# Preparing the second image inside the first maximum pass, and loading x ahead of the weights, in a kernel of two attention layers

## The reference

```python
# layer 0
f = xf @ wf + bf; g = xf @ wg + bg; hh = xf @ wh + bh        # 8, 8 and 64 columns
attn = softmax(einsum('bnk,bmk->bnm', g, f)); o = einsum('bnm,bmc->bnc', attn, hh)
x = gamma * o + x
# layer 1
q, k, v = x @ Wq + bq, x @ Wk + bk, x @ Wv + bv              # 64 columns each
attn = softmax(einsum('bic,bjc->bij', q, k)); out = einsum('bmn,bmc->bnc', attn, v)
x = gamma * out + x
```

## Time and profile before

| | us |
|---|---|
| runs of the kernel before | 4221.15, 4228.95, 4231.31; median 4228.95 |
| profiled execution, its own time | 4228.57 |
| its span | 4226.4 |
| TensorE busy in the span | 4030.3 (95%) |
| VectorE, ScalarE, GpSimd busy | 3271.2, 3191.0, 1953.5 |
| first window of 100 us: TensorE busy | 40.24 |

### The profile page before, as it was taken

One profiled execution on the slowest core, in us unless ns is written; L12 is line 12 of the kernel. 1 busy time (PEld: TensorE's weight loads), 2 busy tenths in 40 slices (PEclk: granted clock), 3 DMA queues, 4 the chain that ended last, 5 costly groups with the idle time before them and its releaser, 6 DMA issues.

```text
span 4226.4 us, 84183 instructions
## 1 busy us (share of the span) xinstructions
PE 4030.3 (95%) x25681; PEld 1349.5 (32%) x25681; DVE 3271.2 (77%) x6298; ACT 3191.0 (76%) x5674; POOL 1953.5 (46%) x909
## 2 busy tenths in 40 slices
PE   4999999999999999999999999999999999999999
PEld 3223332233322333223332233323333233322333
DVE  3877887778877787777877788777887778877787
ACT  2466896778867788767986689776897678977788
POOL 3596106941089311992029910497105961079410
PEclk7799999999999999999999999999999999999999
DMA  1001000010000000000000000001000010000000
GB/s 33 1 1 31 1 1 11 1 31 1 1 12 11 21 1 11 1 11 21 1 12 1 18 14 1 11 1 31 1 1 12 1 31 1 1 11 3 30 1 11
DMA packets 15060, 41.88 MB, mean 10 GB/s; under 512 B 4068, under 2 KB 4068, under 8 KB 12260
## 3 DMA queue, kind: packets, MB, share of 16 engines
q1 hardware_dynamic: 14692, 36.96, 2.9%
HBM read 20.17 MB, written 8.39 MB: 7 GB/s over the span
## 4 chain that ended last, share of the span: by engine, by line
PE 84%; DVE 6%; issue 6%; ACT 3%; POOL 0%; SPq 0%; DVEq 0%; DMA 0%; ACTq 0%; POOLq 0%
PE sum_banks L480 23%; PE sum_banks L578 20%; PE score_banks L566 20%; PE score_banks L466 12%; PE sum_banks L502 3%; PE sum_banks L438 2%; DVE tile_max L922 1%; DVE o_tr L1089 1%; ACT e_whole L816 1%; PE score_banks L430 1%; DVE c_stack L949 1%; ACT g_tr L734 1%; PE sum_banks L415 1%; DVE k_low L969 0%; DVE x_mid L1140 0%
## 5 line engine op out<-in xcount | busy, mean ns | idle before, releaser
L816 ACT ACTIVATE e_whole<-score_banks,exp_bias,down 128x512 f32<-128x512 f32 x2048 | 1573.9, 773 | 249.8 <-DVE o_tr L1089 211.3
L922 DVE TENSOR_REDUCE tile_max<-sum_banks 128x1 f32<-128x512 f32 (+1 forms) x2128 | 1364.8, 685 | 444.0 <-PE sum_banks L438 440.5
L355 POOL TENSOR_TENSOR e_sum<-e_sum,e_whole 128x1024 f32<-128x1024 f32 x704 | 1659.5, 2357 | 83.0 <-ACT e_whole L752 31.9
L752 ACT ACTIVATE e_whole<-score_banks,no_bias,down 128x1024 f32<-128x1024 f32 x1024 | 1229.0, 1204 | 527.1 <-PE score_banks L466 516.1
L1089 DVE TENSOR_SCALAR_CACHE_REDUCE o_tr<-score_banks,neg_down 128x1024 f32<-128x1024 f32 x1024 | 1313.6, 1283 | 320.4 <-PE score_banks L566 281.4
L480 PE MATMUL sum_banks<-e_whole,proj 128*64 128x512 f32 x4096 | 1123.3, 626 | 0.0
L578 PE MATMUL sum_banks<-e_whole,v_scaled 128*64 128x512 f32 x4096 | 1066.7, 602 | 45.1 <-DVE v_scaled L1079 17.1
L566 PE MATMUL score_banks<-k_high,q_split 128*64 128x512 f16 x4096 | 810.2, 388 | 30.6 <-ACT e_whole L816 9.7
L566 PE MATMUL score_banks<-k_low,q_split 128*64 128x512 f16 x4096 | 799.2, 382 | 0.0
L438 PE MATMUL sum_banks<-f_tr,g_tr 33*128 33x512 f16 x2128 | 700.4, 402 | 19.0 <-DVE tile_max L922 14.6
L352 POOL TENSOR_TENSOR e_sum<-e_whole 128x1024 f32<-128x1024 f32 x32 | 75.4, 2357 | 1355.5 <-ACT e_whole L752 1355.5
(11 more groups left out here) (147 smaller groups left out, 1868.5 us busy)
## 6 DMA issues: line engine op xcount, KB each, us to landing
x_in<-in_x_dram SPq DMA_DIRECT2D x19, 1024.0 KB, 4.9
out_dram<-x_mid SPq DMA_DIRECT2D x32, 256.0 KB, 2.7
k_high<-k_high SPq DMA_DIRECT2D x32, 128.0 KB, 2.2
k_low<-k_low SPq DMA_DIRECT2D x32, 128.0 KB, 2.2
w<-in_L_conv_wg_dram SPq DMA_DIRECT2D x2, 2.0 KB
w<-in_L_conv_wf_dram SPq DMA_DIRECT2D x2, 2.0 KB
w<-in_L_conv_wh_dram SPq DMA_DIRECT2D x2, 16.0 KB
b<-in_L_conv_bh_dram SPq DMA_DIRECT2D x1, 32.0 KB
```

What stands on the lines that cost most here:

```text
L355: nc.gpsimd.tensor_tensor(acc, acc, e_whole[:, i % U0, :], ALU.add).then_inc(e_added, 1)
L752: nc.scalar.activation(e_whole[:, i % U0, :].rearrange("p (a n) -> p a n", a=2), score_banks[:, 2 * (i % 2):2 * (i % 2) + 2, :], ACT.Exp, ...
L816: nc.scalar.activation(e_whole[:, u, h * BANK:(h + 1) * BANK], score_banks[:, 2 * (u % 2) + h, :], ACT.Exp, bias=exp_bias[:, u:u + 1], sca ...
L922: nc.vector.reduce_max(tile_max[:, blk, j:j + 1], sum_banks[:, (2 + j % banks) % 4, :], AX_X).then_inc(a_used, 1)
```

## The change

x of image 0 is loaded first, ahead of the weights. TensorE turns it before it waits for the weights, and VectorE copies and scans it before it works on the weights (the function `weights` holds what stood at L867 to L884). VectorE makes the halves of image 0 right after the scan of image 1, and biases and scales image 1 after them. TensorE starts the maximum pass as soon as image 0's stack is turned. VectorE makes the halves of image 1 after four blocks of the pass; GpSimd, whose program is not changed, then fills the stacks; and TensorE turns them in units between the tiles of the last two blocks. ScalarE's program is not changed either.

```diff
+    UNIT_AT = BPC - 2
+    PIECES_AT = BPC // 2
...
+            load(0, 0)
             for col, w_, b_ in ((0, wg, bg), (CK, wf, bf), (GFW, wh, bh)):
...
-            load(0, 0)
...
+            def turn_image(image):
+                pe.wait_ge(x_loaded, 16 * loads(image, True))
+                for r in range(RT):
+                    turn_x(0, x_in, r, score_banks[:, r, :])
+            def project_image(image):
+                for r, pair in enumerate((pair_c, pair_d, pair_a, pair_b)):
+                    pe.wait_ge(xt_dve[0], image * RT + (r + 1 if r < 2 else RT))
+                    project0(r, pair)
+                pe.wait_ge(pj_act, (image + 1) * RT)
+                bound_of_qk(image, score_banks[:, 0, :])
             pe.wait_ge(ident_ready, 1)
+            turn_image(0)
             pe.wait_ge(const_ready, N_CONST)
             pe.wait_ge(w_in, 16 * N_W)
             pe.wait_ge(h_weighted, 2)
...
+            project_image(0)
+            pe.wait_ge(w1s_ready, 1)
+            turn_image(1)
+            project_image(1)
+            pe.wait_ge(w1s_ready, 2)
+            pe.wait_ge(f_stacked, 4)
+            pe.wait_ge(g_stacked, 4)
+            for n in range(UNITS):
+                if n >= 4:
+                    pe.wait_ge(unit_sb, n - 3)
+                turn_stack(n, score_banks[:, n % 4, :])
+            pe.wait_ge(unit_sb, UNITS)
+            for blk in range(BPC):
+                for j in range(ATN):
+                    max_pass_tiles((0, 0, 0), blk, [j], 4)
+                    if blk >= UNIT_AT and j % 2 == 1:
+                        n = (blk - UNIT_AT) * (ATN // 2) + j // 2
+                        if n == 0:
+                            pe.wait_ge(f_stacked, 8)
+                            pe.wait_ge(g_stacked, 8)
+                        if n >= 4:
+                            pe.wait_ge(unit_sb, UNITS + n - 3)
+                        turn_stack(n, score_banks[:, n % 4, :])
+            for blk in range(EARLY):
+                max_pass_tiles((0, 0, 1), blk, range(ATN), 4)
             pe.wait_ge(unit_sb, 2 * UNITS)
-            for chunk, blocks in ((0, BPC), (1, EARLY)):
-                for blk in range(blocks):
-                    max_pass_tiles((0, 0, chunk), blk, range(ATN), 4)
             first_max_rows()
...
             for image in range(2):
                 for r in range(RT):
                     turned_x(image, 0, r, score_banks[:, r, :])
                 scan_x(image)
-                fg_bias(image, image)
                 if image == 0:
+                    weights()
+                    fg_bias(0, 0)
                     fg_largest(0, 0)
-                scales(image, image, score_banks[:, 0, :])
-            for image in range(2):
-                if image == 1:
-                    fg_largest(1, 1)
-                    dve.wait_ge(f_stacked, 4)
-                    dve.wait_ge(g_stacked, 4)
-                fg_scales(image)
-                fg_scaled(image, image)
-                fg_high_part(image, image)
-                fg_rest(image, image)
...
-            with dve.Fori(0, BPC) as blk:
+                    scales(0, 0, score_banks[:, 0, :])
+            fg_scales(0)
+            fg_scaled(0, 0)
+            fg_high_part(0, 0)
+            fg_rest(0, 0)
+            fg_bias(1, 1)
+            fg_largest(1, 1)
+            scales(1, 1, score_banks[:, 0, :])
+            with dve.Fori(0, PIECES_AT) as blk:
+                block_max(0, blk, range(ATN), 4)
+            dve.wait_ge(f_stacked, 4)
+            dve.wait_ge(g_stacked, 4)
+            fg_scales(1)
+            fg_scaled(1, 1)
+            fg_high_part(1, 1)
+            fg_rest(1, 1)
+            with dve.Fori(PIECES_AT, BPC) as blk:
                 block_max(0, blk, range(ATN), 4)
             split_max(0, 0)
```

More of the change, by code:

```diff
@@ L865, in _ @@
             nc.vector.memset(bound_in[C:C1, :], 1.0).then_inc(const_ready, 1)
[L867 to L885, removed]
+            def weights():
+                dve.wait_ge(w_in, 16 * N_W)
+                dve.wait_ge(ident_ready, 1)
+                chain.link(nc.vector.tensor_scalar(w0[:, GFW:PW], w0[:, GFW:PW], gammas[:, 0:1], None, ALU.mult))
+                nc.vector.tensor_scalar(b0[:, GFW:PW], b0[:, GFW:PW], gammas[:, 0:1], None, ALU.mult).then_inc(h_weighted, 1)
+                chain.link(nc.vector.scalar_tensor_tensor(h_abs[:, :], w0[:, GFW:PW], -1.0, w0[:, GFW:PW], ALU.mult, ALU.max))
+                for a in range(2):
+                    rows = slice(a * C, (a + 1) * C)
+                    chain.count(nc.vector.tensor_tensor(mid_abs[rows, :], h_abs[rows, :], ident[rows, rows], ALU.add))
+                chain.link(nc.vector.tensor_scalar(hb_mul[:, :], hb_raw[:, :], gammas[0:C, 0:1], None, ALU.mult))
+                chain.link(nc.vector.scalar_tensor_tensor(bound_in[0:C, :], hb_mul[:, :], -1.0, hb_mul[:, :], ALU.mult, ALU.max))
+                nc.vector.scalar_tensor_tensor(wb_abs[:, :], wb_raw[:, :], -1.0, wb_raw[:, :], ALU.mult, ALU.max
+                                               ).then_inc(h_weighted, 1)
+                dve.wait_ge(coef_ps, 1)
+                nc.vector.tensor_copy(mid_t[:, :], sum_banks[0:C, 0, 0:P]).then_inc(coef_sb, 1)
+                dve.wait_ge(coef_ps, 2)
+                chain.count(nc.vector.reduce_max(x_coef[:, :], sum_banks[:, 1, 0:P], AX_X))
+                chain.link(nc.vector.reduce_max(b_coef_raw[:, :], sum_banks[:, 0, 0:P], AX_X))
+                nc.vector.tensor_scalar(b_coef[:, :], b_coef_raw[:, :], 2.0 ** -100, None, ALU.max).then_inc(coef_sb, 1)
@@ L1016, in _ @@
             dve.wait_ge(const_ready, N_CONST)
-            rebase(START)
             for image in range(2):
@@ L1021, in _ @@
                 scan_x(image)
-                fg_bias(image, image)
                 if image == 0:
+                    weights()
+                    fg_bias(0, 0)
                     fg_largest(0, 0)
-                scales(image, image, score_banks[:, 0, :])
-            for image in range(2):
-                if image == 1:
-                    fg_largest(1, 1)
-                    dve.wait_ge(f_stacked, 4)
-                    dve.wait_ge(g_stacked, 4)
-                fg_scales(image)
-                fg_scaled(image, image)
-                fg_high_part(image, image)
-                fg_rest(image, image)
-            assert chain.n == 2 * (LINK_PIECES + LINK_BOUND)
-            rebase(START + 2 * (LINK_PIECES + LINK_BOUND))
-            with dve.Fori(0, BPC) as blk:
+                    scales(0, 0, score_banks[:, 0, :])
[15 more added lines that the diff above has]
+            with dve.Fori(PIECES_AT, BPC) as blk:
                 block_max(0, blk, range(ATN), 4)
@@ L1041, in _ @@
                 block_max(1, blk, range(ATN), 4)
-            START += 2 * (LINK_PIECES + LINK_BOUND) + LINK_MAX
+            START = chain.n
             def image_steps(image, par):
```

## The result

The changed kernel takes 4204.6 us (median of 5, 4200.1 to 4208.5) against 4225.9 us before (median of 5), a ratio of 0.9948 with a 95% interval of 0.9934 to 0.9963. The forecast was 4201.5. The profiled execution has a span of 4202.5 us, 23.9 less than before.

What follows compares the result with a forecast made beforehand. The prediction took one long chain through TensorE, 95% busy, as the bound, so time saved before the first chunk stays saved. −30.65 + 2.9 + 0.7 = −27.05 us from 4228.57 gave 4201.5 us, own bounds 4196 to 4208, range 4194 to 4213.

Steps and rivals of the forecast that it cites:

- The front: Before the maximum pass: loading and turning x first starts projection 3.6 us earlier and image 0's stack 5.1 us earlier.
- GpSimd's switch back: GpSimd's return from the all-reduce to ordinary operations before image 0's stack: 6.8 us, bounds 5.96 to 8.26.
- start of the pass: The maximum pass begins at 62.8 us instead of 93.45, without waiting for image 1: 30.65 us earlier.
- The halves: After four blocks of the pass VectorE stops its reductions for image 1's halves: 2.9 us added, at most 3.8.
- Rival 1: In the pass, GpSimd's stack operations and VectorE's reductions exclude each other, adding 8.0 us: 4209.5 us; chance 12%.
- The transposes: Eight units of eight between tiles in the pass's last two blocks: 0.7 us added, bounds 0 to 2.4.
- The stack beside the pass: GpSimd finishes image 1's stack at 93.3 to 93.9 us, just before TensorE asks at 93.9; nothing added.
- Rival 2: Ahead of the pass: image 0's stack still starts at 51.2, so 5.1 us are not won: 4206.6 us; chance 10%.
- Rival 3: TensorE's clock stays low in the first chunks, about 28 us per chunk; two chunks give 4258.6 us; chance 3%.
- the mark: Start of the matrix product ending the first chunk's preparation, at 142.86 us before; forecast near 115.8.

Runs made afterwards that it cites:

- the pass alone: Changed kernel with its front put back in the old order and image 1 still in the maximum pass; ratio 0.9952 to the kernel before.
- the spread kernel: Changed kernel with image 1's halves after one block and a unit of transposes behind each sixth tile from the 30th; 4198.1 us, on repeat 4203.5 us.
- the front alone: Changed kernel with image 1's stack made and turned ahead of the maximum pass, as before; ratio 0.9987 to the kernel before.
- the changed kernel's second profile: The changed kernel measured again, unaltered, beside the other experiments; 4210.0 us, ratio 0.9957 to the kernel before.

## Why the prediction was right, and where it was not

*The front.* Forecast 3.6 us for the projection, measured 4.0: the last weight came 0.4 us earlier (18.11), for which I had left 0 to +1, the wrong side. GpSimd's switch back took 7.8 us where I took 6.8 from the one undisturbed row; so the stack started at 46.9 instead of 46.1. Over the runs the same idle time was between 7.7 and 9.0 us. The pass started at 63.58 (forecast 62.8).

*The sum, as measured.* −29.87 (start of the pass) + 0.42 (first reduction 0.96 us behind it instead of 0.54) + 3.55 (halves) + 4.46 (transposes) = −21.44. The 4.46 are the remainder: the 64 reductions take 46.33 us (64.54 to 110.87) where they took 38.36, 7.97 more, of which 3.55 are the halves; the other 0.04 lie between the last reduction and the mark. Forecast were −30.65 + 2.9 + 0.7. The 0.42 had no term in the forecast, and its cause stays open.

*The halves* were 0.65 us above my value and within its bound; the cause is the one I had named as the bound. I had put the exclusion of the two engines on GpSimd's side only, as 0.7 us of waiting. What the runs show is that it can fall on either. VectorE's low half took 1.57 us in all six profiles in which GpSimd's stack operation started within 0.02 us of it, and 0.69 where GpSimd came later or not at all. In the kernel of the pass alone, for image 0, the low half started 0.2 us ahead (50.44 against 50.66) and took 0.69; there GpSimd's pair took 2.38 us instead of 2.03. Which of two nearly simultaneous operations is held the recorded starts don't tell: VectorE's of 4.54 us stands 0.03 us ahead of GpSimd's and waited all the same. The trace agrees with the Trainium skill, "SBUF — State Buffer" (section "SBUF: two separate sides"), which names VectorE operations with two SBUF inputs; the one of 4.54 us has its two inputs from there, and the reductions from PSUM beside the same stack were not stretched. Rival 1 (they take turns for the whole stack) is therefore wrong: 20 reductions took 12.04 us while GpSimd worked.

*The transposes* are the term that was mis-sized: 0.7 forecast, 0 to 2.4 as bounds, 4.5 measured. Two steps of it failed. I let the clock rise once TensorE had no gaps; it stayed at 0.50 through 14.5 us of such work in the changed kernel (96.27 to 110.77), and through 22.8 us in the spread one (82.56 to 105.37). The Trainium skill, "TensorE: Matmul & The Clock Gate" (section "What's actually happening"), by whose rule I would have taken 0, would have been further off; where the page and the rows differ, the rows decide. And I priced transposes and tiles each at their own pace. In turn a unit takes 0.97 us (0.85 in a row of units: 55.86 to 56.71 in the changed kernel), two tiles 0.97 (0.85 by their columns), and six tiles 2.67 (83.53 to 86.20) where 6 × 0.427 are 2.56: about 0.11 us at each change between the two kinds, a price that the rows show and whose cause they don't. So two tiles and a unit are 1.93 us instead of 1.7, and eight times the difference to 1.20 is 5.9 instead of 4.1 (the forecast's 8 × 0.5, which is 4.0), of which 1.4 didn't reach VectorE, where I had left 2 for the filled banks.

*The stack beside the pass* was the step I called a hair's breadth; it held with 2.1 us to spare, since it started 0.5 us later and TensorE 2.4. *Rival 2* (front moves nothing) is wrong by the front alone. *Rival 3* (the clock low in the first chunk) happened a little: it rose some 16 us into the first chunk (which starts at 123.6) instead of 10,

```profile
135.00:140.00 5.00, 5.00 (x18) 0.85 (x16) 2.58 (x4) 2.08 (x2) 4.43 (x2) 0.52 0.00 0
140.00:145.00 5.00, 5.00 (x34) 1.27 (x32) 3.06 (x5) 2.94 (x4) 1.94 (x1) 1.00 0.01 3
```

and the first 30 us behind the mark had a mean clock of 0.69 against 0.79. It never came near the point from which it decides, a whole chunk at the lower level.

*Behind the mark.* The part behind it took, in twelve profiles, from 4073.2 to 4095.9 us (before 4083.5, after 4081.1), with no order by kernel. Two profiles of the spread kernel alone, with marks of 115.53 and 115.61, stand at 4074.5 and 4095.9. So no single median here could have settled a term of the sum. What causes the scatter stays open.

*What was luck.* The forecast gain was 27.05 us; the measured one is 21.44 at the mark and 21.24 by the medians, so the forecast was 5.6 to 5.8 us off. That 4201.5 came out only 3.1 us below 4204.6 is owed to its base: I took the gain off the profiled execution, 4228.57, which lies 2.7 us above the median of five, 4225.85. The mechanism was right (image 1 out of the way, GpSimd's switch ahead of the stack of image 0, a pause for the halves); the price of the transposes was not, and the nearness of the time doesn't speak for it.

## What to carry to other kernels

Work that waits on another engine's slow start belongs inside a stretch that doesn't need it: here moving image 1 into the pass gave 17.7 of 21.4 us. Once it is there, count the host engine's time anew. Transposes between the tiles are nearly free only where the tiles and the unit together fit the other engine's pace (six tiles and a unit nearly did, 3.64 us against 3.59; two tiles and a unit didn't, 1.93 against 1.20). So spread them, and price the changes between kinds of matrix work. And look at what VectorE does while GpSimd starts a long operation: a trivial instruction can carry the full length of it.

## What was not expected of the hardware

- TensorE, waiting for no other engine for 22.8 us, stayed at 1.2 GHz when 33-row tiles and transposes came in turn, with some 0.11 us lost at each change; in a row of transposes alone the clock rose 2.9 us behind the first one in the changed kernel (55.05 to 57.9) and 5.9 in the spread one (54.70 to 60.6). Why it stayed low is not shown.
- One VectorE operation on 128x1 elements took 4.54 us beside a GpSimd operation of 4.49 us, and 0.16 us when GpSimd was held back. In the changed kernel's second profile the same operation and the one behind it took 0.88 and 1.08 us beside GpSimd's first stack operations, where nothing waited for them.
- VectorE wrote the stack pieces in 0.20 us each, by copies, for which GpSimd, multiplying by ones, takes 1.0 us; and VectorE had no switch to wait for.
